# One stream per engine over all phases: layer norms, half sums and the store moved into the phases, and global attention written out

## What is computed

```python
x = x + 0.5 * ffn(layernorm(x))          # call 0: two layers
x = x + attention(layernorm(x))          # global attention, one head, theta = 0.5 + 0.2 sigmoid + 0.15 tanh + 0.1 relu
x = x + 0.5 * ffn(layernorm(x))          # call 1: the same two layers, same weights

def _layer(x, ...):                      # inside ffn, twice per call
    q, k, v = split(shift_token(x) @ wqkv)           # 8 heads of 64
    q, k = rotary(l2norm(q) * qs, l2norm(k) * ks)
    x = x + local_attention(q, k, v) @ wo            # windows of 64 tokens, each sees the one before
    h = layernorm(shift_token(x)) * g + b
    a, g = split(h @ w1 + b1)
    return x + (a * gelu(g)) @ w2 + b2
```

## Time and profile before

| | |
|---|---|
| median of 3 runs | 3387.79 us (3386.68 to 3387.89) |
| the profiled execution | 3386.2 us, of which 3384.1 us are its span |
| PE busy | 3094.7 us (91%) |
| DVE busy | 2744.0 us (81%) |
| ACT busy | 2271.2 us (67%) |
| POOL busy | 1437.8 us (42%) |
| mean granted TensorE clock | 0.970 |

### The profile page before, as it was taken

How to read it: one execution, slowest core, us unless ns; L and a number is a source line. 1 busy time by engine, 2 the same in 40 slices (tenths; PEclk the granted TensorE clock), 3 DMA queues, 4 the chain that set the end, 5 groups by cost and what they waited for, 6 DMA issues and landing times. The chain is left out here.

```text
span 3384.1 us, 83808 instructions
## 1 busy us (share of the span) xinstructions
PE 3094.7 (91%) x30497; PEld 2209.3 (65%) x30497; DVE 2744.0 (81%) x6260; ACT 2271.2 (67%) x5488; POOL 1437.8 (42%) x572
## 2 busy tenths in 40 slices
PE   0899999999999999966999279999999999999997
PEld 0477777666777777634777247777776677777764
DVE  5788988767888888566999768989886798898865
ACT  0588888735888887314888248888873588888732
POOL 1566666404666655010000146666551366666510
PEclk9899999999999999987999679999999999999999
DMA  3111112211111121100000111111211111112212
GB/s 90 38 39 40 41 41 49 49 37 31 41 41 39 40 50 44 26 2 29 14 13 0 38 32 41 41 41 41 47 44 44 25 44 41 41 41 47 47 25 57
DMA packets 176174, 129.65 MB, mean 38 GB/s; under 512 B 85194, under 2 KB 140451, under 8 KB 175779
## 3 DMA queue, kind: packets, MB, share of 16 engines
q1 hardware_dynamic: 175778, 124.39, 15.6%
HBM read 14.24 MB, written 4.19 MB: 5 GB/s over the span
## 5 line engine op out<-in xcount | busy, mean ns | idle before, releaser
L449 POOL TENSOR_TENSOR ffn_rnorm<-ffn_ssq_floor,neg_half 128x16 f32<-128x16 f32 x256 | 745.4, 2912 | 984.6 <-DVE ffn_qkr L685 911.0
L454 POOL TENSOR_TENSOR ffn_qk_cos<-ffn_qk_cos,ffn_qk_sin 128x1024 f32<-128x1024 f32 x256 | 606.9, 2371 | 0.0
L487 ACT ACTIVATE ffn_probs<-psum,ffn_neg_max 128x128 f32<-128x128 f32 x2048 | 584.1, 378 | 22.7 <-DVE ffn_neg_max L661 22.7
L973 PE MATMUL psum<-ffn_wqkv,ffn_hT 128*128 128x512 f32 x1024 | 563.1, 634 | 6.5 <-ACT ffn_hT L502 6.5
L646 DVE TENSOR_TENSOR ffn_qk_sin<-psum,ffn_sin 128x256 f32<-128x256 f32 x1024 | 380.6, 412 | 28.1 <-ACT ffn_sq L494 27.4
L494 ACT ACTIVATE ffn_sq<-psum 128x512 f32<-128x512 f32 x512 | 318.1, 621 | 107.5 <-PE psum L973 107.5
L652 DVE TENSOR_TENSOR ffn_qk_cos<-psum,ffn_cos 128x512 f32<-128x512 f32 x512 | 347.2, 679 | 18.3 <-ACT ffn_sq L494 18.1
L661 DVE TENSOR_REDUCE ffn_neg_max<-psum 128x4 f32<-128x512 f32 x512 | 329.5, 685 | 38.7 <-PE psum L913 35.8
L522 ACT COPY ffn_probsT<-psum 128x512 f32<-128x512 f32 x512 | 276.6, 591 | 110.5 <-PE psum L1013 110.5
L995 PEld LDWEIGHTS psum<-ffn_wo,ffn_oT 128*128 128x128 f32 x2048 | 267.2, 191 | 123.2 <-issue 122.9
L857 PE MATMUL psum<-ffn_zT,ffn_w1g 128*128 128x512 f32 (+1 forms) x768 | 344.3, 593 | 3.1 <-DVE Y L711 1.9
(11 more groups left out here) (137 smaller groups left out, 6196.2 us busy)
## 6 DMA issues: line engine op xcount, KB each, us to landing
ffn_vprev<-ffn_v SPq DMA_DIRECT2D x512, 130.0 KB, 2.4
ffn_ystage<-Y SPq DMA_DIRECT2D x256, 64.0 KB, 2.0
ffn_h<-Y SPq DMA_DIRECT2D x32, 256.0 KB
ffn_h<-Y SPq DMA_DIRECT2D x32, 254.0 KB
X<-in_L_attn_x SPq DMA_DIRECT2D x8, 512.0 KB, 7.1
att_ys<-Y SPq DMA_DIRECT2D x8, 512.0 KB, 2.9
out<-X SPq DMA_DIRECT2D x8, 512.0 KB, 5.9
ffn_wqkv<-in_L_ffn_wqkv SPq DMA_DIRECT2D x4, 768.0 KB, 4.6
```

The costliest lines, as they stand in the source:

```text
L449: nc.gpsimd.tensor_tensor(rnorm[:], ssq_floor[:], neg_half[:], ALU.pow).then_inc(rnorm_ready, 1)
L454: nc.gpsimd.tensor_tensor(both, both, qk_sin[:, t.m % 2, :], ALU.add).then_inc(sum_ready, 1)
L487: last = nc.scalar.activation(probs[:, c * P:(c + 1) * P], bank(3 + i, (c % 4) * P, (c % 4 + 1) * P), ACT.Exp, bias=neg_max[:, c:c + 1])
L973: nc.tensor.matmul(bank(i), hT[:, t.m * P:(t.m + 1) * P], wqkv[:, i * INNER:(i + 1) * INNER], start=True, stop=True).then_inc(qk_psum, 1)
```

## The change

All phases stand in one block; each engine has one stream. One loop, `program`, gives the order for all of them, over four layers (`LAYERS`) and the global attention between layers 1 and 2.

- **Layer norm.** DVE takes a tile's statistics (`moments`); POOL does all the rest (`normalise`: add epsilon, power -0.5, subtract and multiply into Y). Before layers 0 and 2 this is done for 6 tiles ahead, for 2 tiles in each of the four fill slots, and for one tile in each of the attention slots s = 0 to 49. Before the global attention it follows each group's half sum.
- **Half sums.** `half_done` adds Y/2 to X for a group of 4 tiles behind its `residual`, in the MLP slots of layers 1 and 3.
- **The store** of a sequence is issued in the MLP slots of layer 3, the last one at the end.
- **Global attention** is written out. The folding of its weights and the projection of its first sequence (`FIRST`) are laid into the last six MLP slots of layer 1; in those, the gates use two pairs of banks and leave banks 0 and 1 to them. Layer 1's last group is combined in its slots k = -1 and 0. The fill slots of layer 2 are laid over its last slots, k = 63 to 66 (`early_tile`). `th_full` takes the place of `mix`.
- **Staging.** `ystage` and `ys` are gone: PE transposes Y itself. In layer 0 the fill slots use banks 6, 5 and 2, which are free then.
- **Start.** The first sequence, the identity, the tables, scales and projections are loaded first, then the second sequence, the masks and the gates, then the rest of x. Nothing is loaded again at layer 2 but the weights, and that in layer 1's first MLP slot.

```diff
+        def program(local_slot, mlp_slot, global_slot):
+            for L in range(LAYERS):
+                for s in range(-4 if L == 0 else 0, NT + 2):
+                    local_slot(L, s)
                 for g in range(1, NG):
                     mlp_slot(L, g)
+                if L == DEPTH - 1:
+                    for k in range(-1, NT + 3):
+                        global_slot(k)
...
+        def early_tile(k):
+            return k - NT - 3
...
+        FIRST = {NG - 6: [("w", 0)], NG - 5: [("w", 1)], NG - 4: [("x", 0), ("x", 1)], NG - 3: [("p", 0), ("p", 1)],
+                 NG - 2: [("o", 0), ("o", 1)], NG - 1: [("o", 2)]}
...
+        def two_pairs_from(L):
+            return NG - 4 if over(L) else NG - 6 if L < LAYERS - 1 else NG
...
         def x_bank(t):
-            return 1 if t.row < 5 else 6
+            return 1 if t.L and t.row < 5 else 6
...
+        def norm_units(L, s):
+            lo = 2 * (s + 4) + 6
+            if L % DEPTH:
+                return None
+            if s < 0:
+                return range(lo, lo + 2)
+            return range(s + 14, s + 15) if 0 <= s and s + 14 < NT else None
...
 # SP
+            load_rows(0)
+            sp.dma_start(ident[:], id_in).then_inc(ident_in, 16)
+            sp.dma_start(rot[:], rot_in.rearrange("t (m p) d -> p t m d", p=P)).then_inc(consts_in, 16)
+            load_scales(0)
+            load_projections(0)
+            load_rows(1)
+            sp.dma_start(mask32, mask_in.rearrange("t p c -> p t c")).then_inc(consts_in, 16)
+            load_gates(0)
+            for b in range(2, B):
+                load_rows(b)
+            sp.wait_ge(consts_done, 3)
+            program(local_slot, mlp_slot, global_slot)
+            store(B - 1)
+            sp.wait_ge(stored, 16 * B)
...
 # POOL
+            def normalise(T, rows):
+                n, q = len(rows), T % 8
+                pool.wait_ge(ln_var, T + n)
+                nc.gpsimd.tensor_scalar(ln_rstd[:, q:q + n], ln_moments[:, q:q + n, 1], 1e-5, None,
+                                        ALU.add).then_inc(ln_eps, 1)
+                units.append(T)
+                pool.wait_ge(ln_eps, len(units))
+                nc.gpsimd.tensor_tensor(ln_rstd[:, q:q + n], ln_rstd[:, q:q + n], neg_half[:, 0:n],
+                                        ALU.pow).then_inc(ln_root, 1)
+                pool.wait_ge(ln_root, len(units))
+                for i, row in enumerate(rows):
+                    nc.gpsimd.tensor_scalar(Y[:, row, :], X[:, row, :], ln_moments[:, q + i, 0:1],
+                                            ln_rstd[:, q + i:q + i + 1], ALU.subtract, ALU.mult).then_inc(ln_ready, 1)
...
+            def local_slot(L, s):
                 if t := tile_at(L, s + 4):
                     root(t)
                     total(t)
+                if rows := norm_units(L, s):
+                    normalise(2 * NT * (L // DEPTH) + rows[0], rows)
...
 # DVE
+            def moments(T, rows):
+                for i, row in enumerate(rows):
+                    wait(dve, ln_var, T + i - 7)
+                    nc.vector.bn_stats(ln_stats[:, (T + i) % 8, :], X[:, row, :]).then_inc(ln_stat, 1)
+                for i, row in enumerate(rows):
+                    dve.wait_ge(ln_stat, T + i + 1)
+                    wait(dve, ln_ready, T + i - 7)
+                    nc.vector.bn_aggr(ln_moments[:, (T + i) % 8, :], ln_stats[:, (T + i) % 8, :]).then_inc(ln_var, 1)
...
+            def half_done(t):
+                done = t.L // DEPTH * NG + t.row
+                dve.wait_ge(y_ready, t.n + 1)
+                xs, ys = (a[:, t.row * GROUP:(t.row + 1) * GROUP, :].rearrange("p m d -> p (m d)") for a in (X, Y))
+                nc.vector.scalar_tensor_tensor(out=xs, in0=ys, scalar=0.5, in1=xs, op0=ALU.mult,
+                                               op1=ALU.add).then_inc(half_ready, 1)
+                if t.L < LAYERS - 1:
+                    dve.wait_ge(half_ready, done + 1)
+                    moments(NT + t.row * GROUP, range(t.row * GROUP, (t.row + 1) * GROUP))
...
                 if t := tile_at(L, s + 4):
                     keys(t)
+                if rows := norm_units(L, s):
+                    if L == 0:
+                        dve.wait_ge(loaded[rows[0] // MT], 16)
+                    else:
+                        dve.wait_ge(x_ready, rows[-1] + 1)
+                    moments(2 * NT * (L // DEPTH) + rows[0], rows)
...
 # PE, mlp_slot
+                pieces = first_pieces(L, g)
                 gates(t, 0)
...
+                if pieces:
+                    prepare(0, *pieces[0])
                 gates(t, 1)
...
+                if len(pieces) > 1:
+                    prepare(0, *pieces[1])
                 combine(group_at(L, g - 1))
...
 # PE, global_slot
+                if early_tile(k) >= -4:
+                    local_slot(DEPTH, early_tile(k))
```

More of the change, by code:

```diff
@@ new lines, in macaron @@
+        probsT = shared[:, 6 * N:7 * N]
+        probs = shared[:, 7 * N:8 * N]
+        hid01 = shared[:, 8 * N:10 * N].rearrange("p (i c n) -> p i c n", i=2, c=2)
+        mask32 = probs.rearrange("p (t c) -> p t c", t=2)
+        gate = [probs[:, 0:GCOLS], probs[:, GCOLS:2 * GCOLS], gate2]
+        hid = [hid01[:, :, 0, :], hid01[:, :, 1, :], hid2[:]]
+        two = lambda lo: shared[:, lo * N:(lo + 2) * N].rearrange("p (i n) -> p i n", i=2)
+        th_half, th_full, theta, g_probs, g_probsT = (two(2 * i) for i in range(5))
@@ L536, in normal @@
                 wait(act, ag_psum, 3 * t.n)
-                nc.scalar.copy(zT[:], bank(7 if t.row else 0)).then_inc(zT_ready, 1)
+                nc.scalar.copy(zT, bank(7 if t.row else 0)).then_inc(zT_ready, 1)
             def gated(t, c):
@@ L606, in _ @@
-            for w in range(2):
-                nc.vector.tensor_tensor(windows16[:, w * WIN:(w + 1) * WIN], ident[:, 0:WIN], ident[:, WIN:P],
-                                        ALU.add).then_inc(consts_done, 1)
-            dve.wait_ge(consts_in, 32 * call + 32)
-            nc.vector.tensor_copy(mask[:], mask32).then_inc(consts_done, 1)
             def tables(L):
@@ L813, in mlp_slot @@
                     statistics(L, (g + 3) // 2)
-                if g == 6 and over(L):
+                if g == 6 and L < LAYERS - 1:
                     tables(L + 1)
-            def close(L):
-                residual(group_at(L, NG - 2))
-                residual(group_at(L, NG - 1))
-                dve.wait_ge(y_ready, NG * (L + 1))
-            tables(layers[0])
-            slots(attention_slot, mlp_slot, close)
+                for kind, i in first_pieces(L, g):
+                    prepare(0, kind, i)
@@ new lines, in _ @@
+            nc.vector.memset(hid2[:], 1.0).then_inc(consts_done, 1)
+            dve.wait_ge(ident_in, 16)
+            nc.vector.tensor_copy(ident16[:], ident[:]).then_inc(consts_done, 1)
+            for w in range(2):
+                nc.vector.tensor_tensor(windows16[:, w * WIN:(w + 1) * WIN], ident[:, 0:WIN], ident[:, WIN:P],
+                                        ALU.add).then_inc(consts_done, 1)
+            dve.wait_ge(consts_in, 32)
+            tables(0)
+            nc.vector.tensor_copy(mask[:], mask32).then_inc(consts_done, 1)
@@ L917, in tokens_transpose @@
             def tokens_transpose(t):
-                pe.wait_ge(staged[t.m % 4], 16 * (t.n // 4 + 1))
-                if x_bank(t) == 6:
+                if t.L % DEPTH == 0:
+                    pe.wait_ge(ln_ready, 2 * NT * (t.L // DEPTH) + t.row + 1)
+                else:
+                    pe.wait_ge(y_ready, (t.L - 1) * NG + t.row // GROUP + 1)
+                if x_bank(t) == 6 and t.row < 5:
+                    wait(pe, hT_ready, before(t, 1, 2))
+                elif x_bank(t) == 6:
                     wait(pe, probsT_ready, 2 * (t.n - 5) + 1)
@@ L968, in project_qk @@
                     wait(pe, kT_ready, before(u, 0, 2))
-                elif u := tile_at(t.L, t.row - 2):
-                    wait(pe, v_ready, before(u, 0))
+                elif t.row == 2 and t.L:
+                    wait(pe, v_ready, t.n - 1)
+                elif t.row == 0 and t.L == DEPTH:
+                    pe.wait_ge(theta_ready, NT - 1)
                 else:
@@ L1031, in queries_transpose @@
             def queries_transpose(t):
-                if t.row < 2:
+                if t.row < 2 and t.L:
                     pe.wait_ge(rot_ready, 6 * (t.n + 3))
+                elif t.row < 3:
+                    wait(pe, qT_ready, before(t, 1))
                 elif u := tile_at(t.L, t.row - 3):
@@ L1254, in prepare @@
                         wait(pe, vo_ready, 3 * n)
[L1255 to L1256 removed]
                     for m in range(4 * i, 4 * i + 4):
[L1258 removed]
+                        last = nc.tensor.transpose(bank(b, (m % 4) * P, (m % 4 + 1) * P), Y[:, MT * n + m, :], ident[:])
                     last.then_inc(xT_psum, 1)
```

806 lines of the change are left out of this document (366 added, 440 removed).

## The result

| | before | after |
|---|---|---|
| median of 4 runs | 3387.23 us (3386.47 to 3387.89) | 3175.88 us (3174.11 to 3177.26) |
| the profiled execution, and its span | 3386.2, 3384.1 us | 3177.26, 3175.5 us |
| PE, DVE, ACT, POOL busy | 3094.7, 2744.0, 2271.2, 1437.8 us | 3081.3, 2697.3, 2268.3, 1674.1 us |

The ratio is 0.938 (95% interval 0.936 to 0.939): 6.2% faster. I had forecast 3195 us and a range of 3176 to 3242; the time lies 19 us under the forecast and 0.1 us under the range. The profiled execution is the slowest of the four, 1.4 us above their median.

What follows compares the result with a forecast made beforehand. PE was taken to bound the slots at 8.54 us, DVE the attention, with about 316 us at the seams; terms of -65, +8, -61.5, +2, -63 and -11.5 sum to -191, from 3386.2 to 3195 us, range 3176 to 3242.

Steps and rivals of the forecast that it cites:

- the staging transfers: Steady part: removing the 256 transfers was put at nothing, because PE hid them and nothing waits for them there.
- Start: Before layer 0's steady slots: earlier masks and a shorter fill bring the first scores to 54, 65 us less (58 to 70).
- Steady slots: Layers 0 and 2, 50 slots each: slack covers the moments, POOL's unit fits; 8 us more (0 to 45) for extra waits.
- rival B: Steady slots of layers 0 and 2: POOL's norm and qkr collide, 30 to 45 us, 3225 to 3240; chance 21%.
- Layer 1 into attention: Between layer 1 and the global attention: serial prologue and transfers go, first mix at 1509.2; 61.5 us less (54 to 66).
- Attention: Global attention: same instructions in the same order, plus moments of two tiles in three slots; 2 us more.
- Attention into layer 2: Gap after the attention: first transpose right behind tile 61's values, fill of 47 us; 63 us less (55 to 66).
- End: Kernel's end: only last residual, one half sum and one store remain, ending at 3373; 11.5 us less (9 to 13).
- C: Start and seams: only serial DVE and SP work goes, prologues and fills keep their length; 130 us, 3256; chance 12%.
- D: Slots 0 to 49 of layers 0 and 2: POOL's `normalise` becomes the bound, slower than before, up to 3477 us; chance 3%.

Runs made afterwards that it cites:

- e1: The kernel before, with its local attention transposing Y directly, without the 256 staging transfers and PE's wait for them; 3362.93 us, ratio 0.993.
- e7: The changed kernel, with DVE's reciprocal, scaling and addition for the attention's last three tiles one slot earlier, ahead of the local step; 3165.46 us.
- e9: e7 with layer 2's fill using the banks of layer 0's fill, each behind its last use in the attention; 3155.19 us.
- e4: The changed kernel, with two more bn_stats of the tile behind the moments in the 100 slots that normalise one tile; 3189.72 us.
- e3: The changed kernel, with POOL's 128-column multiply of the norm issued once more in the 100 slots that normalise one tile; 3195.89 us.
- e6: The changed kernel, in layer 1's MLP slots: half sum and its moments behind DVE's third product, PE's second piece behind combine; 3172.88 us.
- e5: The changed kernel, with layer 2's four fill slots behind the global attention's last slot instead of laid over its end; 3171.98 us.
- e2: The kernel before, with the second and third transfer of h exchanged, the single-partition one issued first; 3389.65 us, ratio 1.001.
- e12: The changed kernel, with two one-column adds on POOL ahead of the norm's multiply in the 100 slots that normalise one tile; 3174.55 us.

## Why the prediction was wrong, and where it was right

The direction, the places and nine tenths of the size were right. The step that failed is the one that put the staging transfers at nothing: "PE hid them, and nothing waits for them in the steady part: nothing." I had looked at slots in the middle of a layer. In the last slots of each layer PE did wait, 13.8 us by the kernel before's own list of waits (144.4 us in 14 waits for `ystage`, which I read as the two seams), because the staging transfer stood on SP's queue behind an issue of 16.2 us (the rows at e1), and e1 wins 14.8 us there. With those 14 us the forecast would have been 3181 us, 5 us above the time. That it then comes so near is partly luck: of the other terms, three were short of the gain, by 8.0, 2.4 and 2.6 us, and three over it, by 2.8, 0.5 and 6.7 us. By the other terms:

- *Start*, 65 forecast, 67.4 measured. The masks landed by 18.5 (17 to 22), queries at 21.7 (23.4), the first mask matmul at 50.75 (54). 4.2 us of it are the staging's landing (e1), which the forecast had no term for, so the size came out better than its parts. PE waits for POOL's norm once, for the first tile (8.9 us), and never after it. Layer 0's fill by itself moves by 3.3 us with the granted clock (e7, e9), more than the term's error of 2.4.
- *Steady slots*, +8 forecast, 0 measured. The mechanism, a loop with slack, and its slack of 0.5 to 0.7 us were right (e4: 0.61), so the 0.08 us a slot "for extra waits" had no ground; the term is 8 us of the error. I also placed the norm's multiply beside qkr; it is done 0.18 us before. That took rival B's ground away, not its rule: with one multiply more it cost 20 us (e3).
- *Layer 1 into attention*, 61.5 forecast, 58.7 measured. The stalls were 8.84 us for 8, but from the slots with eight tiles' statistics and from hand-overs; the gates' stalls are not from the half sum (e6). The first mix also stands behind the last combine: DVE waits 1.79 us for it.
- *Attention*, 2 forecast, 2.5 measured.
- *Attention into layer 2*, 63 forecast, 56.3 measured. I took 3 us for two drains in the fill; the fill is 52.6 us for the 47 forecast, because of the waits from DVE's order and the lower clock in the same stretch (e7). The forecast took something off for a higher clock; it was 0.72 over this fill for 0.61 before, and of the 9.8 us that e7 wins there 5.7 are matmuls at the higher level. That interleaving the drain is worth nothing (e5), no rival had.
- *End*, 11.5 forecast, 14.1 measured: 5.1 us from the last residual to the end (3170.42 to 3175.5) for 19.15 (3364.95 to 3384.1). The forecast's own end, 3373, gives 11.1.

Of the rivals, C (fills keep their length, 3256) was half right in mechanism and wrong in size: layer 2's fill was longer than before, and layer 0's took 41.8 us for 45.4; but the norms and loads ahead of them went as planned. D is excluded by POOL's unit of 1.80 us.

## What to carry over

Before pricing a removed transfer at nothing, take the list of waits and subtract the large ones you already explain: what is left (here 13.8 us in twelve waits) is the part that the middle of a stage doesn't show, and it stood where large transfers were issued on the same queue. When two phases are laid over each other, write out every engine's order inside the shared slots: here a drain whose result is made behind the next phase's step left the overlap worth nothing (e5), and its order (10.4 us) and the banks (some 10 us) were worth more. Of what a stretch with waits loses, part can be the granted clock (5.7 of the 9.8 us in e7), so compare busy time and idle time of the same instructions and not the waits alone. The lead of one instruction that comes once a tile, before minus after, shows in one column where a change of this size won its time. It also shows what a stretch that wasn't changed gains or loses by itself, up to 3.4 us here.

## What was not expected of the hardware

- Behind the two large transfers of h (256 and 254 KB, in pieces of 256 bytes) the next issue on SP's queue takes 15.4 to 16.9 us, whichever transfer it is (both kernels and e1 at 32 places, e2 at 16).
- POOL's 128-column multiply takes 0.80 us, a power of one column 0.58, an add of one column 0.24. Issued just behind qkr, the multiply takes 1.81 (e3); with 0.42 us or less of it left when qkr starts, neither is longer (e12).
- `ssq_floor`, 16 columns, takes 0.17 us in the fill with POOL idle, 1.01 in e4 and 1.49 in e3, the last two to the end of POOL's `total`. In the kernel before it ends 0.03 us behind a POOL instruction in 240 of 256 tiles.
- In layer 2's fill PE's granted clock was 0.59 over the stretch with the waits of 2.00 and 4.90 us, and 0.92 over the first three steps without them (e7).
- The same code in layer 0's fill ran at a granted clock of 0.87 in e7 and 1.00 in e9 and took 3.3 us less in e9.
